# Hypergraph layer of a two-layer graph kernel: the first product's operands exchanged, dn multiplied into u, relu's output made transposed at once, its variance from a mean of squares; other orders at both ends

## The reference, cut to what matters

```python
h = relu(layernorm(x))                     # no gain, eps 1e-5
H = (adj != 0)                             # 512 x 512
Dn = H @ w;  Dn = where(Dn > 0, 1/Dn, 0)   # w: adj's first row
Be = H.sum(axis=0);  Be = where(Be > 0, 1/Be, 0)
# first conv
m = Be[:, None] * (H.T @ (h @ W1.T))
r = relu(Dn[:, None] * (H @ m) + b1)       # 512 x 512
# layer norm of r with gamma, beta, then second conv
n = (r - mean(r)) * rsqrt(var(r) + 1e-5) * gamma + beta
g = Be[:, None] * (H.T @ (n @ W2.T))
x1 = x + h + Dn[:, None] * (H @ g) + b2
# second layer
X = relu(layernorm(x1));  a = adj * exp(leaky_relu(sj + si + ab))
P = a / (a.sum(-1) + 1e-12)
out = x1 + relu(X@Wk0 + (P@X)@Wk1 + (P@P@X)@Wk2 + sum(bk))
```

## Time and profile before

| | |
|---|---|
| median of 3 runs | 832.19 us (831.83 to 833.0) |
| the profiled execution's own time | 833.39 us |
| its span (first to last instruction) | 831.6 us |
| instructions | 16643 |
| granted PE clock, mean | 0.994 |
| one steady turn | 49.27 us |
| DMA | 57.83 MB, 70 GB/s in the mean |

### The profile page before, as it was taken

The page is one execution under the profiler, slowest core; times in us unless marked ns, Lnnn a source line. Parts: engine busy times, 40 slices in busy tenths (PEclk is TensorE's granted clock), DMA queues, the critical chain, the costliest instruction groups (busy, mean ns, idle before and its releaser), DMA issues.

```text
span 831.6 us, 16643 instructions
## 1 busy us (share of the span) xinstructions
PE 807.6 (97%) x5752; PEld 752.7 (91%) x5752; DVE 643.2 (77%) x1726; ACT 475.7 (57%) x1006; POOL 428.8 (52%) x595
## 2 busy tenths in 40 slices
PE   6888999999999999999999999999999999999997
PEld 5777999999899998999999999999989999898986
DVE  6877887778887777887778788777878777777565
ACT  4436657384674838557483755738366473854644
POOL 4666363654826366382645737365473636542242
PEclk9998999999999999999999999999999999999999
DMA  8411204022040312204022130402204040110000
GB/s 296 122 64 52 89 1 151 16 77 89 0 164 0 118 46 68 95 0 164 0 79 85 30 134 0 158 6 76 88 0 164 0 131 34 52 51 1 26 21 32
DMA packets 39856, 57.83 MB, mean 70 GB/s; under 512 B 2576, under 2 KB 21008, under 8 KB 39824
## 3 DMA queue, kind: packets, MB, share of 16 engines
q1 hardware_dynamic: 39104, 57.42, 20.8%
q10 hardware_dynamic: 720, 0.01, 0.0%
HBM read 49.03 MB, written 8.39 MB: 69 GB/s over the span
## 4 chain that ended last, share of the span: by engine, by line
PE 90%; DVE 5%; ACT 2%; issue 1%; POOL 1%; ACTq 0%; DVEq 0%; POOLq 0%
PE ps L757 85%; PE ps L953 3%; PE ps L898 1%; PE ps L942 1%; DVE hw L1095 1%; DVE r_sb L1211 0%; POOL p_lo L470 0%; DVE st_r L1217 0%; DVE st_x L1086 0%; ACT e_sb L619 0%; DVE part_b L1265 0%; DVE inc L1110 0%; DVE x L1323 0%; DVE part_a L1116 0%; ACT e_sb L625 0%
## 5 line engine op out<-in xcount | busy, mean ns | idle before, releaser
L757 PE MATMUL ps<-w_hi,part_a 128*128 128x256 f32 (+1 forms) x512 | 158.0, 344 | 8.1 <-DVE part_a L1116 6.8
L453 POOL TENSOR_TENSOR y<-y,bk_row 128x256 f32<-128x256 f32 x64 | 56.4, 911 | 206.8 <-DVE a_lo L1241 206.8
L757 PE MATMUL ps<-w_lo,part_a 128*128 128x256 f32 (+1 forms) x384 | 123.6, 322 | 0.0
L757 PEld LDWEIGHTS ps<-w_hi,part_a 128*128 128x128 f32 x512 | 97.4, 190 | 21.9 <-DVE part_a L1116 8.5
L757 PE MATMUL ps<-wk_hi,xt_hi 128*128 128x258 f32 (+1 forms) x256 | 89.4, 349 | 3.3 <-DVE xt_lo L1141 1.8
L757 PE MATMUL ps<-wk_hi,xt_lo 128*128 128x258 f32 (+1 forms) x256 | 86.7, 338 | 0.0
L757 PE MATMUL ps<-wk_lo,xt_hi 128*128 128x258 f32 (+1 forms) x256 | 86.5, 338 | 0.0
L1235 DVE TENSOR_TENSOR e_sb<-e_sb,adjt_sb 128x512 f32<-128x512 f32 x64 | 44.2, 690 | 44.9 <-ACT e_sb L625 44.9
L757 PEld LDWEIGHTS ps<-w_lo,part_a 128*128 128x128 f32 x384 | 73.3, 191 | 5.8
L457 POOL TENSOR_TENSOR xt_lo<-xl,xt_hi 128x256 fp32r<-128x256 f32 x60 | 56.5, 970 | 31.8 <-ACT xt_hi L699 31.8
L693 ACT ACTIVATE p_hi<-y 128x256 fp32r<-128x256 f32 x60 | 23.9, 419 | 85.2 <-DVE y L1285 85.2
(11 more groups left out here) (150 smaller groups left out, 2532.4 us busy)
## 6 DMA issues: line engine op xcount, KB each, us to landing
adj_sb<-in_adj SPq DMA_DIRECT2D x30, 512.0 KB, 5.6
adjt_sb<-in_adj_t SPq DMA_DIRECT2D x15, 1024.0 KB, 5.3
xin<-in_x SPq DMA_DIRECT2D x15, 512.0 KB, 4.6
out_dram<-x SPq DMA_DIRECT2D x15, 512.0 KB, 3.4
w_row<-in_adj SPq DMA_DIRECT2D x16, 256.0 KB, 3.4
adjt_sb<-in_adj_t SPq DMA_DIRECT2D x4, 256.0 KB, 6.9
e_sb<-in_w_t SPq DMA_DIRECT2D x2, 512.0 KB, 7.9
y<-in_wk SPq DMA_DIRECT2D x3, 256.0 KB, 7.4
```

Of the source, the lines that this page charges most:

```text
L453: pool.tensor_tensor(y10[:, t, D:], y10[:, t, D:], bk_row[:, :], ALU.add).then_inc(po_y0, 1)
L757: return pe.matmul(dst, stationary, moving, start=first, stop=last, skip_group_check=True)
```

## The change

- The first product is turned round: W1's blocks are stationary and u, transposed, is moving, so that z and relu's output have hidden features on partitions and need no transposes (the 16 of L953 and their copies are gone). relu with the bias b1, a column now, reads PSUM directly on ACT and writes `r_sb[:, f]`; `r_hi_of` and `lo_of_r` split it into part_b and part_a.
- The row factor dn can't be applied to z any more and is taken into u: PE transposes dn's columns, broadcast, into a row in PSUM (`dn_across`), ACT copies it to `dn_row` (the tile hw), DVE multiplies (`u_f`, into r_sb's first two tiles), and u's high and low parts are made from there. dn is computed one step ahead, between the parts of m.
- The variance of r: w2_hi has two more columns of 1/512, so that y's product gives the mean; DVE squares the four tiles (`square`, into e_sb), adds them in pairs (`add_squares`) and together (`sum_of_squares`), and four one-column products (`squares`) sum over partitions between y_tile(1) and y_tile(2). `var_of_r(h)` on DVE forms mean of squares minus square of the mean for two tiles at a time, POOL clamps it at 0, adds eps and takes the power, for each pair. stats_r and norm_r are gone.
- y's parts go to p_hi and p_lo (in the last step with a first layer: h_hi and h_lo), since part_a holds r's low part.
- Orders: on ACT the four spreads stand ahead of y10_out; h_of(t) stands behind relu(t); on POOL the fourth addition stands ahead of rs_r; on DVE the order of the diff below.
- Head: batch 0's w comes as a column by an ACT DMA and PE sums it (`sum_ps`) instead of DVE's four sums; b1 is loaded as columns; wk_lo waits for x1; u_f and u_lo of batch 1 stand between x1's tiles and statistics. End: the last steps' variance of x1 goes in pairs, two high parts of a are made by DVE, one tile of v moves, two matmuls that only kept the clock up are left out.

The diff, cut to its core:

```diff
@@ SP, head
-            load_w_row(Step(0, 0), 0)
@@ POOL, step (the last wait: k == 0, ahead of wk_lo)
                 if s.prev2 and s.prev:
                     for t in range(TI - 1, TI):
                         wait(pool, ac_v, at(s, -2, t))
                         pool.tensor_tensor(x1[:, q, t, :], y10[:, t, D:], x1[:, q, t, :], ALU.add).then_inc(po_out, 1)
+                if s.here:
+                    for h in range(2):
+                        pair = slice(2 * h, 2 * h + 2)
+                        wait(pool, dv_vr, at(s, 0, 2 * h + 1))
+                        pool.tensor_scalar(v_r[:, 1, pair], v_r[:, 0, pair], 0.0, EPS_LN, ALU.max,
+                                           ALU.add).then_inc(po_vr, 2)
...
+                        pool.tensor_tensor(rs_r[:, pair], v_r[:, 1, pair], minus_half[:, pair],
+                                           ALU.pow).then_inc(po_rsr, 2)
...
+                    wait(pool, dv_x1, at(s, 0))
@@ ACT, step
+                    wait(act, pe_dn, at(s, 0))
+                    act.activation(dn_row[:, :], dn_ps, ACT.Copy).then_inc(ac_dn, 4)
                     for d in range(TD):
+                        wait(act, dv_uf, at(s, 0, 2 * d + 1))
+                        act.activation(part_a[:, d, :], r_sb[:, d, :], ACT.Copy).then_inc(ac_u, 2)
...
+                        act.activation(r_sb[:, f, :], ps0[:, f, :], ACT.Relu, bias=b1_c[:, f:f + 1]).then_inc(ac_relu, 1)
...
+                        act.activation(part_b[:, f, :], r_sb[:, f, :], ACT.Copy).then_inc(ac_r, 1)
...
+                    x_of(0), x_of(1), x_of(2), x_of(3), relu(0), h_of(0), relu(1), h_of(1), relu(2), h_of(2)
+                    r_hi_of(0), relu(3), xt_of(0), xt_of(1), h_of(3)
+                    relu_v(0), relu_v(1), r_hi_of(1), y2_of(0), y2_of(1), relu_v(2), y2_of(2), relu_v(3), y2_of(3)
+                    r_hi_of(2), r_hi_of(3)
+                spread(0..3), y10_out(0), exp(0), y10_out(1), exp(1), exp(2), y10_out(2), hi_of_a(0), exp(3)
+                y10_out(3), hi_of_a(1), hi_of_a(2), y_hi(0), y_hi(1), eps_of_rows(), hi_of_a(3), y_hi(2), y_hi(3)
@@ PE, step
+                    wait(pe, dv_mlo, at(s, 0))
+                    if s.prev2:
+                        wait(pe, dv_p, at(s, -2))
+                    dn_across()
...
+                            mm(ps0[:, f, :], w1_hi[:, d, col(f)], part_a[:, d, :], d == 0, False)
+                            mm(ps0[:, f, :], w1_hi[:, d, col(f)], part_a[:, TD + d, :], False, False)
+                            last = mm(ps0[:, f, :], w1_lo[:, d, col(f)], part_a[:, d, :], False, d == TD - 1)
...
-                            last = pe.transpose(ps0[:, t, col(c)], r_sb[:, t, col(c)], ident[:, :])
...
+                    for t in range(TI):
+                        last = mm(sq_ps[:, t, 0:1], r_sb[:, 0, col(t)], ones_c[:, 0:1], True, True)
+                    last.then_inc(pe_sq, 4)
...
+                    y_tile(0), y_tile(1), squares(), y_tile(2), y_tile(3)
@@ DVE, step
+                        dve.tensor_tensor(r_sb[:, d, :], ps0[:, d, :], dn_row[:, :], ALU.mult).then_inc(dv_uf, 2)
...
-                        dve.tensor_tensor(part_a[:, TD + d, :], ps0[:, d, :], f32(part_a[:, d, :]),
+                        dve.tensor_tensor(part_a[:, TD + d, :], r_sb[:, d, :], f32(part_a[:, d, :]),
                                           ALU.subtract).then_inc(dv_ulo, 2)
...
+                        dve.tensor_tensor(e_sb[:, f, :], r_sb[:, f, :], r_sb[:, f, :], ALU.mult).then_inc(dv_add, 1)
...
+                        dve.tensor_tensor(e_sb[:, f, :], e_sb[:, f, :], e_sb[:, f + 1, :], ALU.add).then_inc(dv_add2, 2)
...
+                        dve.tensor_tensor(part_a[:, f, :], r_sb[:, f, :], f32(part_b[:, f, :]),
+                                          ALU.subtract).then_inc(dv_rlo, 1)
...
+                    u_f(0), incidence(0), incidence(1), u_f(1), u_lo(0), shift of x, u_lo(1), sums(0)
+                    v_tile(0), square(0), v_tile(1), square(1), square(2), add_squares(0), square(3), lo_of_xt(0)
+                    add_squares(2), lo_of_xt(1), lo_of_r(0), sum_of_squares(), v_tile(2), v_tile(3), lo_of_y2(0..3)
+                    si, sj, sj_mid, lo_of_r(1), lo_of_r(2), lo_of_r(3), sums(1), mult_a(0), mult_a(1), incidence(2)
+                    mult_a(2), lo_of_a(0), incidence(3), mult_a(3), lo_of_a(1), var_of_r(0), lo_of_a(2), y_lo(0), y_lo(1)
+                    lo_of_a(3), var_of_r(1), sums(2), stats_x(0, 2), y_lo(2), y_lo(3), sums(3)
```

679 lines of the change are left out of this document (381 added, 298 removed).

## The result

The changed kernel takes 959.2 us in the median of 4 runs (956.5 to 962.5), the kernel before 832.6 in the same job: ratio 1.152, 95% interval 1.150 to 1.154. The forecast was 917 in a range of 822 to 950: right in direction and, for the steady step, in mechanism, but too small by 42 us and outside the range. The profiled execution has a span of 954.7 (before 831.6), so 123.1 us are to be explained.

The account below looks back on a forecast made before the run. PE's own instructions were taken to bound the steady steps, if other engines deliver in time. 0.5 + 2.7 + 4.0 - 0.4 = +6.8 us a step, 13 steps +88: 833.4 + 88 - 3 = 918.4, median 917, range 822 to 950.

Parts of the forecast that it names:

- The ends: Start, second batch and end of the kernel: added and removed work together -3 us, between -10 and +4.
- the late variance: Steady step, DVE and POOL: r's row factor now comes after y, making y_lo(3) ready at T 43.7, wanted at 39.7.
- PE's own work: Steady step on PE: transposes removed, dn transposes and squares' products added, together -0.4 us a batch.
- Exclusion: DVE's two-SBUF-operand instructions and POOL's take turns: 6.0 us together, POOL's last addition at T 26.3 instead of 21.3.
- (a): Rival, half of it: DVE and POOL meet only in part, last addition T 23.3, step +3.8, 878 us; chance 0.15.
- Landing: Load of adj's second half, behind POOL's last addition: lands at T 33.1, bounds 27.1 and 33.5, 6.8 after POOL's end.
- m: Steady step, PE's next-incidence stage: waits for incidence(3), a stall of 2.7 us.
- g: Steady step, PE's g_stage: waits for y_lo(3), a stall of 4.0 us.
- Small ones in front: Steady step, before m: u_lo(1) about 0.2 and y2 copies about 0.3, together 0.5 us, bounds 0 and 1.5.
- The clock: PE in steady steps: stalls may bring the lower clock; taken as 0, upper bound 22 us over 13 steps.
- (c): Rival, faster: PE stays the bound and everything is hidden, 823 us; chance 0.24 with its edge.
- (b): Rival, no port effect, only the late variance: +0.9 us a step, 841 us; chance 0.14.

Follow-up runs that it names:

- e6: Changed kernel with two edits at its start: first batch's sums of w on DVE as before, wk_lo no longer waiting for x1; 962.1 us, ratio 1.156.
- e18: e17 plus filler matmuls in two PE waits of the first batch (before the first product, and in g); 871.2 us, ratio 1.046.
- e8: Kernel before, with the second batch's u_lo and x1's tiles put ahead of the statistics on DVE; 835.3 us, ratio 1.003.
- e10: Changed kernel: adj's second half loaded first, variance early, 13 two-operand instructions made one-operand bn_stats, second batch's incidence ahead of squares; 861.5 us, ratio 1.036.
- e4: Changed kernel with 30 filler matmuls of 256 columns in PE's wait for y_lo in g; 934.6 us, ratio 1.122.
- e1: Changed kernel with the load of adj's second half issued on SP ahead of the store and load of x; 901.3 us, ratio 1.082.
- e7: e1 with DVE's order changed behind exp so that the variance comes earlier, nothing left out; 890.2 us, ratio 1.070 to the kernel before.
- e5: Changed kernel with adj's second half loaded first and 13 two-operand DVE instructions replaced by one-operand bn_stats; 876.4 us, ratio 1.052.
- e9: Kernel before with four bn_stats of relu's output replaced by two-operand squares written into hw, waits added, variance constant; 848.6 us, ratio 1.020.
- e15: Kernel before with six small memsets added on DVE at the end of each step; 832.4 us, ratio 1.000.
- e2: Changed kernel with the row variance of relu's output left out and y scaled by 1; 863.8 us, ratio 1.036.
- e11: Kernel before with DVE's second batch reordered: statistics first, then u_lo, last two sums of w, rest of dn, z tiles; 832.4 us, ratio 1.000.
- e16: Kernel before with four bn_stats of relu's output replaced by squares written over the same tile, code no longer, variance constant; 835.3 us, ratio 1.004.
- e13: Changed kernel with its loop over pairs of batches written out; 958.9 us, ratio 1.149.
- e17: Changed kernel with e7's edits, sums of w on DVE, second batch's incidence ahead of squares, loop written out, nothing left out; 873.1 us, ratio 1.048.

## Why the prediction was wrong, step by step

**The step that failed is "The ends": "Together I take -3, between -10 and +4."** Head, second batch and the rest measure +20.0, +6.2 and -0.8, so +25.4 where the forecast had -3. That is 28 of the 38 us by which the span missed the sum (+123 against +85); without it the time would have been in the range. I had listed the additions to the head (+0.5, +3.2, +2) and set against them four DVE sums and a wait, as if it were throughput; but the head is one chain. What the runs put in its place: sums of w on PE and the extra DMA on ACT's queue 5.8 (e6). The other 14 is read from e6's milestones against the kernel before and not tried one by one, so its causes are argued: the first product is still 4.9 later by the way dn, transposes, copy, u_f, u_lo; y's own stretch is 4.4 longer, at clock 0.70 (how much of it is clock stays open, see e18); g is 2.9 longer, waiting for y_lo behind the late variance, which I had counted in the steady steps and forgotten here; 2.2 at the end, since the next batch's transposes of dn now wait for dn. For the second batch I forecast a gain from an early u_lo. The early start came (T 7.4 for 9.9), the gain did not, and e8 shows none from it either (the second step 55.8 for 53.9). What makes that batch 6.2 longer is not shown; e10's order takes 3.6 off it in a kernel with one-operand instructions.

**PE's own work, -0.4: right in its parts.** The transposes of dn take 0.36 (0.44 forecast), the squares 0.81 (0.81).

**Exclusion: right, milder.** I let every instruction take its worst turn and had the last addition at T 26.3; it ends at 23.5, which is rival (a)'s 23.3. Sums and low parts take 1.0 to 1.2 as forecast, squares 0.86, u_lo 0.72. I had let only DVE's two-operand instructions and POOL's next one meet, and did not look at how many operands POOL's has: its h_hi, with one, waits too, 408 to 772 ns.

**Landing: T 31.3 against 33.1,** in its bounds (27.1 to 33.5); from POOL's end it took 7.8 and not 6.8, which gave part of the milder exclusion back.

**Stalls in the steady step.** m: 2.7 forecast, 0.5 us in all 13 steps measured. g: 4.0 forecast, 3.6 a step measured. Small ones in front: 0.5 forecast with a bound of 1.5; measured 1.1 for si and, at each of five returns of the loop, about 1 for u_lo, 0.4 a step. Together PE is idle 66.2 us in 13 steps, 5.1 a step, and busy 2.4 a step more than before. Of these 2.4, 1.8 are the clock (e4), forecast 0; the rest, 0.6, I have not taken apart (in e1 and e7, at clock 1.00, it is 0.4 a step). So 7.5 a step is measured and 6.8 was forecast. The steady part alone (97.7 against 88, upper bound 110) would have been well inside the range. The near hit is partly luck: m was too large by 2.7, the clock too small by 1.8 and si not priced. Two sums in the forecast are off by 0.1 each (33.1 + 1.9 is 35.0, and the terms from incidence(3) to y_lo(3) add up to 8.7); they cancel in T 43.7. It ended at T 42.4.

**The clock.** The mechanism stood in the text ("stalls of 2.7 and 4.0 us in each step may bring the lower clock too") and was priced at 0 because no steady row showed it. The row that did exist, half clock after the 6.1 us idle in the earlier trace rows, was the nearest one and should have decided.

**The rivals.** (c) falls by the result. (b) describes e5 (no exclusion, load in time): it pays 1.2 a step in the steps without a return of the loop, where (b) said 0.9, but the changed kernel has the exclusion. (a) was right on POOL's end (T 23.3) and wrong on the step (+3.8, measured +7.5).

**What to carry to other kernels.** Price the ends of a kernel as the one chain they are, milestone by milestone, not as sums of busy time: a step inserted there costs its whole length and its handovers. Delays in one chain are not shares of the loss: what they free one by one is no sum, so ask of each what stands behind it. And where a stall of several microseconds is forecast in each turn, price the lower clock behind it.

## What the runs showed that I had not expected

**A loop's return can stall an engine.** DVE idles 2.5 us at each of the five returns, and the instruction queue moves 25 or 26 more packets, in e9, e15, the changed kernel and all its looped forms but e2; never in the kernel before, e2, e8, e11 and e16. Counting DVE's and its sequencer's records, two steps of the loop hold 284 in the kernel before, 290 in e2, and 296 or 306 where it stalls; from the program's start to the loop's first branch back it is 562, 571 and 580 to 615. Length and place were not varied one without the other but once: e6 has the changed kernel's 306 and ten more records ahead of the loop (615 for 605), and idles 1.6 to 1.9 us more at each return. So the place in the program has a part in the price; whether it decides that there is a stall wasn't tried. The Trainium skill has the rule, page "Runtime: NRT & Kernel Launch", section "Instruction fetch mechanics": a taken branch whose target is not among the two pages held must fetch it before execution goes on. The trace agrees, with 2.5 us as its price; the change's 22 more DVE records a pair were a question to ask before.

**Its price depends on who waits.** 0.8 us in all in e15, 1.9 at each return in e7, and nothing gained by its removal in e13.

**A square of one tile counts as two operands** (964 ns for POOL's skips in e16), and POOL's one-operand copy h_hi waits like its additions (664 ns there, 408 before).

No version beat the kernel before. Nearest is e11, the same within 0.2%; the best form of the change that leaves nothing out, e18, is 4.6% slower (e17 4.8%, their intervals overlap).
